# The next slot's scores in front of the next group's projection, in attention over queries

## What is computed

```python
def _L0_xattn_ref(KV, Q, Wq, bq, Wk, bk, Wo, bo):
    q = (Q @ Wq + bq).reshape(b, q_len, H, HD)          # H = 16 heads of HD = 8
    k = (KV @ Wk + bk).reshape(b, kv_len, H, HD)
    v = k
    scores = jnp.einsum('bqhd,bkhd->bhqk', q, k) / jnp.sqrt(jnp.float32(HD))
    attn = jax.nn.softmax(scores, axis=-2)              # over the queries
    ctx = jnp.einsum('bhqk,bkhd->bqhd', attn, v).reshape(b, q_len, D)
    return ctx @ Wo + bo
```

## Time and profile before

| | us |
|---|---|
| median of 3 runs | 1544.52 |
| lowest, highest run | 1540.27, 1552.53 |
| profiled execution | 1553.07 |
| its span | 1551.1 |
| mean granted clock of TensorE | 0.893 of full |
| busy: PE, DVE, ACT, POOL | 1314.0, 1214.4, 1057.0, 762.1 |

### The profile page before, as it was taken

The page is one execution under the profiler, slowest core; times in us unless marked ns, Lnnn a source line. Parts: engine busy times, 40 slices in busy tenths (PEclk is TensorE's granted clock), DMA queues, the critical chain, the costliest instruction groups (busy, mean ns, idle before and its releaser), DMA issues.

```text
span 1551.1 us, 63503 instructions
## 1 busy us (share of the span) xinstructions
PE 1314.0 (85%) x26438; PEld 863.5 (56%) x26438; DVE 1214.4 (78%) x2629; ACT 1057.0 (68%) x2244; POOL 762.1 (49%) x1558
## 2 busy tenths in 40 slices
PE   5888889898877777777667779999999999999897
PEld 2455556555544444444333346667666666666685
DVE  2556666666546888897899969999999999999755
ACT  2465666676655888876666667777777777777545
POOL 2335445455444777777788843344333332332123
PEclk9789999999877989996565679999999999999878
DMA  7000000000000000000000000000000000000012
GB/s 195 17 3 3 3 3 3 3 4 3 2 9 8 24 17 24 17 16 17 1 1 1 1 1 3 3 3 3 4 3 10 24 17 17 24 17 10 2 42 69
DMA packets 28671, 24.27 MB, mean 16 GB/s; under 512 B 3677, under 2 KB 23907, under 8 KB 28387
## 3 DMA queue, kind: packets, MB, share of 16 engines
q1 hardware_dynamic: 28386, 20.21, 4.6%
HBM read 15.94 MB, written 4.19 MB: 13 GB/s over the span
## 4 chain that ended last, share of the span: by engine, by line
PE 41%; issue 23%; POOL 22%; DVE 7%; ACT 6%; SPq 0%; POOLq 0%; DMA 0%; DVEq 0%; ACTq 0%
PE keys_T L590 7%; PE keys_O L571 5%; POOL gla_low L1156 4%; PE keys_O L577 4%; PE keys_E L485 3%; PE keys_S L331 3%; POOL cross_pairs L837 3%; POOL gla_yg L1180 3%; POOL cross_spread L804 2%; PE keys_E L528 2%; ACT keys_pT L657 2%; POOL gla_sq L1173 2%; PE keys_O L597 2%; DVE ffn_hh L1994 2%; ACT keys_vz L648 1%
## 5 line engine op out<-in xcount | busy, mean ns | idle before, releaser
L657 ACT ACTIVATE keys_pT<-keys_T 128x512 f32<-128x512 f32 x256 | 152.3, 595 | 76.5 <-PE keys_T L590 73.1
L340 POOL TENSOR_SCALAR keys_spread<-keys_kT,keys_heads 128x512 f32<-128x512 f32 x128 | 86.8, 695 | 231.1 <-ACT keys_kT L621 231.1
L350 DVE TENSOR_REDUCE keys_mx<-keys_S 128x16 f32<-128x1024 f32 x128 | 156.2, 1220 | 16.6 <-PE keys_S L331 14.9
L590 PE MATMUL keys_T<-ident_sb,keys_pexp 128*128 128x128 f32 x1024 | 165.4, 284 | 3.2 <-ACT keys_pT L657 2.3
L353 DVE TENSOR_TENSOR keys_pe_in<-keys_S,keys_mx 128x1024 f32<-128x1024 f32 x128 | 156.8, 1225 | 4.4
L590 PEld LDWEIGHTS keys_T<-ident_sb,keys_pexp 128*128 128x128 f32 x1024 | 113.0, 141 | 72.8 <-ACT keys_pT L657 38.3
L673 ACT ACTIVATE keys_pexp<-keys_pe_in 128x1024 f32<-128x1024 f32 x128 | 134.7, 1053 | 0.0
L710 DVE RECIPROCAL keys_rinv<-keys_O 128x128 f32<-128x128 f32 x128 | 120.4, 941 | 0.2 <-issue 0.2
L1616 DVE COPY_PREDICATED gla_at<-gla_node,gla_GP 128x256 f32<-128x256 int32 x128 | 64.8, 506 | 70.8 <-ACT gla_at L1470 67.5
L1173 POOL TENSOR_TENSOR gla_sq<-gla_o 128x512 f32<-128x512 f32 x32 | 33.2, 1039 | 138.2 <-ACT gla_o L1478 138.2
L571 PEld LDWEIGHTS keys_O<-keys_pT,keys_vz 128*32 128x32 f32 x4096 | 63.0, 109 | 64.1 <-ACT keys_pT L657 63.7
(11 more groups left out here) (285 smaller groups left out, 3744.0 us busy)
## 6 DMA issues: line engine op xcount, KB each, us to landing
context<-in_ctx_T SPq DMA_DIRECT2D x32, 256.0 KB, 2.6
xs<-in_x SPq DMA_DIRECT2D x8, 512.0 KB, 7.4
out_x<-xs SPq DMA_DIRECT2D x16, 256.0 KB, 2.3
keys_mask_q<-keys_mask_b SPq DMA_DIRECT2D x64, 1.0 KB
keys_bias_right_f<-in_alibi_right SPq DMA_DIRECT2D x1, 512.0 KB, 3.9
ffn_w<-in_L_ffn_w_gate_T SPq DMA_DIRECT2D x1, 256.0 KB, 4.5
ffn_w<-in_L_ffn_w_up_T SPq DMA_DIRECT2D x1, 256.0 KB, 4.7
ffn_w<-in_L_ffn_w_down_T SPq DMA_DIRECT2D x1, 256.0 KB, 5.3
```

The costliest lines, as they stand in the source:

```text
L350: nc.vector.tensor_reduce(m, quads(S), X, ALU.max).then_inc(c["mx"], 1)
L590: last = nc.tensor.transpose(T[:, j * P:(j + 1) * P], pexp[:, t % 2, (4 * half + j) * P:(4 * half + j + 1) * P], sh.ident[:, :])
L657: nc.scalar.activation(pT[:, t % 2, 4 * half:4 * half + 4, :].rearrange("q n k -> q (n k)"), T[:, :], ACT.Copy).then_inc(c["pT"], 1)
```

## The change

In TensorE's list the scores of tile n+1 are issued at the end of slot n, behind the weighting of tile n-2, and no longer at the head of slot n+1. The very first scores stay where they were. Since the early part 2t+1 comes behind the second half, the scores now stand in front of it.

```diff
             def first(g, p, t):
-                if n := back(g, p, t, 0):
-                    scores(*n)
+                if g == 0 and t == 0:
+                    scores(g, p, t)
                 if n := back(g, p, t, 3):
                     output(*n)
 
             def second(g, p, t):
                 if n := back(g, p, t, 2):
                     weigh(*n)
+                if n := back(g, p, t, -1):
+                    scores(*n)
```

## The result

The changed kernel takes 1559.92 us (median of 4 runs, 1551.10 to 1565.61), the kernel before 1544.15 (median of 4). The ratio is 1.0092, with a 95% interval of 1.0051 to 1.0132: 15.8 us by the medians. Measured once more beside the kernel before, it was 1559.11 against 1544.00, ratio 1.0100 (1.0068 to 1.0132). Both intervals lie above 1: the kernel is slower, by about 1%. The forecast was 1556, with the largest chance on "within 1%".

The account below looks back on a forecast made before the run. It took VectorE to bound two slots of four and a loop through ScalarE or the direct exponentials the others. Terms 5.7 (steady groups), 2 (clock) and 3.9 (drain) gave +11.6 us on the median 1544.52: 1556, range 1543 to 1567.

Parts of the forecast that it names:

- rival A: The forecast itself: the scores' long loop through ScalarE gets a second slot per group, +5 to +15 us; chance 0.56.
- D: Slower by over 15.4 us: low clock in the two projection slots makes the long loop dearer, about 1567; chance 0.20.
- Slot 0 to 1: Step to the scores of a group's second tile: they start when the direct exponentials end, gain 0.10 us.
- Slot 1 to 2: Step to the third tile's scores, query projection now behind the scores before: 4.03 us where it was 4.04.
- Slot 2 to 3: Step to the fourth tile's scores, key projection now behind the scores before: 3.93 us for VectorE's 3.47, loss 0.46.
- Slot 3 to 0: Step with the key transposes behind the scores: ScalarE waits 0.4 us, next scores ready at about 3.4, cost 0.06.
- Sum per group: The four steps of a group behind the drain together: +0.41 us, so +5.7 for 14 groups.
- The drain: Stage's first slots: `gla_OUT` 2.18 us later, tile 3's first minimum 495.9 for 491.99; +3.9 us, bounds +1.1 and +6.
- The clock: Groups behind the drain: 1.2 GHz for 16% of the time, 1.4 us more per slot; +2 us, bounds 0 and 3.1.
- What would show it: Profile signs: steps near 4.0, 3.9, 3.45, 3.9, projection evictions waiting; wrong if VectorE's score waits fall below 15 us.
- C: Faster: VectorE's 24 waits for the scores, 21.0 us, go away, about 1525 us; chance 0.05.
- B: Nothing: the ends cancel through ScalarE slack in slot 2 or a cheap drain, -4 to +5 us, about 1545; chance 0.19.

Follow-up runs that it names:

- key_slot_only: Kernel before, with only the scores behind the key projection moved in front of it in groups 1 to 14: 1547.28 us against 1543.66, ratio 1.0010.
- all_but_key_slot: Kernel before, with scores from slot 3 on passing the query projection and the transposes but not the key projection: 1558.77 us against 1543.66, ratio 1.0075.
- drain_only_2: Kernel before, with scores one slot ahead only at the end of slots 0, 1 and 2, the drain: 1550.59 us against 1543.66, ratio 1.0044.
- drain_slot0: Kernel before, with only tile 1's scores moved ahead at the end of slot 0; one traced execution, tile 4 29.4 us behind tile 0.
- drain_slot2: Kernel before, with only tile 3's scores moved ahead at the end of slot 2; one traced execution, tile 4 31.5 us behind tile 0.
- steady_only: Changed kernel with the drain's old order kept, scores one slot ahead only from slot 3 on: 1553.76 us against 1544.00 before, ratio 1.0066.
- again: The changed kernel without an edit, measured once more beside the kernel before: 1559.11 us against 1544.00, ratio 1.0100.
- evict_late_steady: Kernel before, with scores ahead from slot 3 on and ScalarE's early-part evictions moved behind the direct exponentials from group 2's on: 1521.89 us against 1544.00, ratio 0.9860.

## Why the prediction was right, point by point

The time, 1559.9, lies 4 us above the forecast and in its range. The mechanism is that of rival A: the long loop through ScalarE got a second slot. By size the result stands on the seam between A (+5 to +15) and D (above 15.4): +15.8 and +15.1 by the medians. That the forecast came so near is in part luck, since its three terms were off by different amounts, as below: the steady groups by 2 us too little, the drain by about 1 too much, and the clock's +2 stands for -1.2 to +10.5 in single executions.

- **Slot 0 to 1**: forecast -0.10 per group, measured +0.05 (4.01 for 3.96). I let the scores start 0.05 behind the last direct exponential. They start 0.15 behind it, in the changed trace (658.52) as before (653.91 behind 653.76, rows 4, 5). So there was nothing to gain there, and the 0.10 had no ground.
- **Slot 1 to 2**: forecast 4.03, measured 4.06. The eviction was to start 1.81 behind the scores and starts 1.79 behind them. The 4.04 that it was compared with belongs to a group whose slot 0 had been lengthened (its step is 4.69); in full-clock groups this step is 4.13, so it became 0.07 shorter and not 0.01.
- **Slot 2 to 3**: forecast 3.93, measured 3.96 for 3.46. This is the step that decides, and key_slot_only and all_but_key_slot show that it does so as a part of the loop and not as a price of its own.
- **Slot 3 to 0**: forecast 3.45, measured 3.46. ScalarE waits 0.34 for the transposes, as the 0.4 of the text.
- **Sum per group**: +0.41 forecast, 15.50-14.95 = +0.55 measured, so 7.7 us for 14 groups where 5.7 was forecast. Slot 0 is 0.15 worse than forecast, slot 2 by 0.04; slot 1 is 0.06 better. (A slot of the kernel before lasts 3.88 us on average over tiles 5 to 60, by the first minima; the 3.84 of the text divides a window that begins inside a slot.)
- **The drain**: +3.9 forecast, +2.7 in the changed trace (27.7 for 25.0 to tile 3); to tile 4 the four traces of the new order have a mean of 31.2 against 28.0 of the old order, +3.2, with the clock differing among them. `gla_OUT` was to be 2.18 later and is 7.12-4.76 = 2.36 later; the drain's transposes 3.4, measured 20.41-16.82 = 3.59 (481.66 less 461.25, and 482.58 less 465.76); the last `gla_OUT` 4.0, measured 24.76-22.05 = 2.7 (486.01 less 461.25, and 487.81 less 465.76).
- **The clock**: forecast +2, between bounds of 0 and 3.1. The term was mis-sized. Against its full-clock steps the low clock cost the kernel before 6.5 us in groups 2 to 14 (200.8 us for 13 x 14.95) and 1.4 in group 1; three more traces with its order in groups 2 to 14 (drain_only_2, drain_slot0, drain_slot2) have 6.4 to 6.7 there. In the order of the change it cost 0.3, 1.6 and 13.7 us in groups 2 to 14 (the changed kernel, steady_only, again), and 6.4, 6.4 and 4.7 in group 1 (21.9, 21.9 and 20.2 us, at granted clocks of 0.57, 0.57 and 0.75 for 0.92; what the drain leaves in that group is counted with it). The differences against the kernel before are -1.2, +0.1 and +10.5 us: a term that two runs of one kernel put 12 us apart. A slot at 1.2 GHz was to take 1.4 us more and takes 2.0 (5.95 for 3.96). I priced only TensorE's projection and scores; weighting and output grow too, 0.86 to 1.19 and 0.49 to 0.80, and no slack is left for any of them.
- **What would show it**: the waits of `cross_qT` and `cross_kT` (0.82) and the steps were as described. But VectorE's waits for scores fell to 13.3 us, below the 15 that I had named as the sign of being wrong, with the loop at work all the same. The wait had split: `cross_h` waits for the output projection first and gets 6.4 us, which the wait for the scores then lacks. 19.7 us together at a granted clock of 0.99, against 21.4 before at 0.92. A bound on one wait of a loop was the wrong test; one on the period of the loop would have held.
- **The rivals**: C, by the Trainium skill's rule (Perfetto Trace Analysis, Optimization Strategy) to find the fullest engine's gaps and make what they wait for start sooner, did not come: the gaps named the scores, and the scores were a part of the loop, not its cause. The time it gave, 1525, was reached with the edit on ScalarE beside it (1521.9); so the gaps had been the right prize, and the releaser's name the wrong handle. D's mechanism was at work in part, as the clock term shows; the medians stayed below its 1567. B's case, that the ends cancel, failed with the third step.

What stays open is why the low clock, which lengthened one slot at a time in the kernel before, can cover two or three in a row in the changed order (the stretches of 19.6 and 14 us above), and why it was nearly absent from groups 2 to 14 in one execution of the changed kernel and not in the other. One such slot of the kernel before, a step of 6.25 us with 3.46 behind it:

```profile
696.30:702.50 6.20, 5.91 (x89) 3.14 (x89) 3.37 (x8) 4.07 (x15) 4.62 (x10) 0.50 0.01 4
```

TensorE's waits of about 1 us for `cross_oT` stand in the long loop in either order, and no run holds them fixed while the clock changes.

## What to carry to other kernels

Before moving an instruction in front of another on one engine, look up who reads what is passed, and what stands behind that reader on its own list. Work in front of the scores and work behind them, in front of what the next scores need, belong to the same loop; moving it across only hands it on to the next turn. In this kernel it left the loop only when both ends did, the projection behind the scores and its eviction behind the exponentials, and each move alone lost. In a hand-written order, place an eviction where its engine waits anyway.

## What the runs showed of the hardware

What a low clock costs depends on the order as much as on the clock. In groups 2 to 14 the granted clock was 0.92 in the kernel before, 0.91 in the run again and 0.98 in evict_late_steady. With two levels, 1.2 and 2.4 GHz, that makes an estimated 32, 39 and 7 us at the low level, and they cost 6.5, 13.7 and 0.6 us against the full-clock steps: about 0.20, 0.35 and 0.09 us for each microsecond at the low level. What counts is whether a slot at the low level is covered by work of another engine. In the loop it takes 5.95 us instead of 3.96. In evict_late_steady, where the slots are VectorE's, the two stretches at a low clock behind group 1 held steps of only 3.79 and 4.08 for 3.46; their windows:

```profile
618.80:622.60 3.80, 3.60 (x87) 2.35 (x88) 3.45 (x8) 2.90 (x12) 3.44 (x9) 0.58 0.02 4
632.90:636.90 4.00, 3.76 (x87) 2.69 (x88) 3.33 (x8) 3.47 (x14) 3.54 (x9) 0.57 0.03 6
```

And a small thing that shifted one term: the scores start 0.14 to 0.15 us behind the end of the accumulator's read that releases them. In the changed kernel, ScalarE:

```profile
658.16 0.22 ACT L973 ACTIVATION_READ_ACCUMULATOR cross_pexp<-cross_S,cross_least 128x1 f32 x1
```

It ends at 658.38, the scores start at 658.52; in the kernel before 653.76 and 653.91.
